# Gating on unnormalised rows: centred gate weights, a mean column and one rstd chain in a GNN and expert kernel

## What is computed

```
x = x + gnn(layernorm(x))          # two graph convolutions, batch norm over rows, + identity, relu
n = layernorm(x)                   # (x - mean) / sqrt(var + 1e-5), per row
logits = n @ gate_w + gate_b       # 256 x 8
p = softmax(logits); the two largest of 8 keep their p as weights, the others 0
x = x + sum over experts e of p[e] * (gelu(n @ W1[e] + b1[e]) @ W2[e] + b2[e])
```

## Time and profile before

| | |
|---|---|
| runs timed | 2361.3, 2357.24, 2357.84 us; median 2357.84 |
| profiled execution | 2363.68 us, its span 2361.9 us |
| busy | TensorE 82%, GpSimd 70%, VectorE 40%, ScalarE 18% of the span |
| memory traffic | 438.37 MB, 186 GB/s |

### The profile page before, as it was taken

How to read it: one execution, slowest core, us unless ns; L and a number is a source line. 1 busy time by engine, 2 the same in 40 slices (tenths; PEclk the granted TensorE clock), 3 DMA queues, 4 the chain that set the end, 5 groups by cost and what they waited for, 6 DMA issues and landing times.

```text
span 2361.9 us, 30351 instructions
## 1 busy us (share of the span) xinstructions
PE 1928.7 (82%) x8786; PEld 1400.5 (59%) x8787; DVE 933.1 (40%) x2598; ACT 423.6 (18%) x1137; POOL 1650.7 (70%) x1651
## 2 busy tenths in 40 slices
PE   1044592999999997867999999999983838999998
PEld 1044351666566665644666666666652828999997
DVE  7999310222222234422223232333237793333332
ACT  1800100000000001100000000000004673444443
POOL 0777777777777777775777777777756556666675
PEclk6555796999999999977999999999986559999999
DMA  9994542666666654444666656665672246888895
GB/s 325 342 333 130 191 125 55 201 197 206 190 198 206 201 159 149 149 118 145 197 188 192 194 186 194 187 197 182 194 234 80 78 146 174 214 208 210 209 215 127
DMA packets 289701, 438.37 MB, mean 186 GB/s; under 512 B 41634, under 2 KB 225163, under 8 KB 289451
## 3 DMA queue, kind: packets, MB, share of 16 engines
q1 hardware_dynamic: 207979, 268.31, 34.9%
q0 software_dynamic: 79872, 166.48, 27.5%
q10 hardware_dynamic: 1728, 2.13, 0.3%
HBM read 341.71 MB, written 96.51 MB: 186 GB/s over the span
## 4 chain that ended last, share of the span: by engine, by line
POOL 54%; issue 18%; PE 16%; DVE 7%; DMA 3%; ACT 1%; SPq 0%; POOLq 0%; DVEq 0%; ACTq 0%
POOL arena L597 43%; POOL pair_weights L582 11%; PE psum L1724 7%; PE psum L1732 6%; DMA out_dram<-ACC 2%; PE psum L1715 1%; DVE edge_cols L1248 1%; DVE stats L1254 1%; DVE X L1251 1%; ACT ACC L816 1%; DVE ACC L1368 1%; DMA arena<-conv_rows,edge_cols 1%; PE psum L1674 0%; PE psum L1508 0%; DVE ACC L1243 0%
## 5 line engine op out<-in xcount | busy, mean ns | idle before, releaser
L597 POOL DMA_INDIRECT arena<-conv_rows,edge_cols x1064 | 1019.9, 959 | 340.7 <-issue 324.0
L1549 PE MATMUL psum<-arena,X 128*128 128x448 f32 x1960 | 821.5, 545 | 41.0 <-DMA arena<-pair_weights 28.0
L1599 PE MATMUL psum<-arena 128*128 128x256 f32 x2128 | 583.8, 391 | 113.4 <-DMA arena<-conv_rows,edge_cols 109.2
L1599 PEld LDWEIGHTS psum<-arena 128*128 128x128 f32 x2128 | 401.7, 195 | 333.1 <-issue 275.1
L1549 PEld LDWEIGHTS psum<-arena,X 128*128 128x128 f32 x1960 | 375.3, 192 | 267.2 <-issue 218.5
L1178 DVE TENSOR_TENSOR ACC<-ACC,psum 128x256 f32 x76 | 32.1, 422 | 910.4 <-PE psum L1567 910.4
L582 POOL DMA_INDIRECT pair_weights<-scale_b,mean_b x252 | 257.0, 1020 | 132.8 <-issue 76.5
L1157 DVE TENSOR_SCALAR arena<-iota,edge_cols 128x128 f32<-128x128 f32 x1064 | 281.2, 359 | 0.4 <-DVE ACC L1084 0.2
L663 POOL DMA_INDIRECT out_dram<-ACC x105 | 166.5, 1586 | 103.8 <-DMA out_dram<-ACC 86.5
L746 ACT ACTIVATE arena<-psum 128x256 f32<-128x256 f32 x76 | 29.0, 382 | 1033.4 <-PE psum L1599 1033.4
L1724 PE MATMUL psum<-ACC,arena 128*128 128x128 f32 x1680 | 205.7, 275 | 0.2 <-DVE ACC L1395 0.2
(11 more groups left out here) (307 smaller groups left out, 1375.1 us busy)
## 6 DMA issues: line engine op xcount, KB each, us to landing
arena<-pair_weights SPq DMA_DIRECT2D x469, 224.0 KB, 3.4
arena<-in_L_ffn_W_dram SPq DMA_DIRECT2D x113, 512.0 KB, 7.5
pair_weights<-zeros SPq DMA_DIRECT2D x5, 10976.0 KB, 73.1
arena<-conv_rows,edge_cols POOLq DMA_INDIRECT x1064, 2.9
conv_rows<-X SPq DMA_DIRECT2D x13, 896.0 KB, 5.9
X<-in_x_dram SPq DMA_DIRECT2D x12, 896.0 KB, 11.2
rows_for_experts<-ACC SPq DMA_DIRECT2D x7, 910.0 KB, 4.3
out_dram<-X SPq DMA_DIRECT2D x6, 896.0 KB
```

The costliest lines, as they stand in the source:

```text
L597: pool.indirect_dma_start(G[:, n * D:(n + 1) * D], None, y_tab[layer], bass.IndirectOffsetOnAxis(srcT[:, t:t + 1], 0)).then_inc(gathered[n ...
L1549: ins = m.matmul(bank(6 + c, BW), X[:, t * D + c * P:t * D + (c + 1) * P], table, start=(t == 0), stop=(t == NT - 1))
L1599: ins = m.matmul(bank(2 * (k % 2), D), S[:, n * P:(n + 1) * P], G[:, n * D:(n + 1) * D], start=(j == 0), stop=(j == GT - 1))
```

## The change

`SCALED` goes from 4 to 3. The `bn_stats`, `bn_aggr`, root, reciprocal and normalisation per chunk go away, and so do their tiles. TensorE transposes the rows of `X` as they are, after `lb_used`. The gate weights are centred (for each expert, the mean over the 256 features is taken off each weight; the sum over features is made by TensorE against `ones`) and get a ninth column of 1/256, so that a row times them gives the eight products of the centred row and the row's mean. ScalarE squares each tile of `X` into scratch columns of `arena` and sums along the row (`accum_out`, into `ssq`). After `logit_done` one chain on VectorE makes variance = sum/256 - mean^2 for all 49 tiles, one root on ScalarE, and the products are multiplied by 1/root before the bias is added. The row numbers of the four empty adds move into column 1 of `flag_i`, written by GpSimd just before them.

```diff
-SCALED = 4
+SCALED = 3
...
+        no_row = flag_i[:, 1:2]
...
+        NC = NX + 1
+        gate_mean = sb("gate_mean", KC * NC)
+        squares = [G[:, 4 * KC * H + n * D:4 * KC * H + (n + 1) * D] for n in range(12)]
...
-                g.iota(no_row[:, :], [[0, 1]], base=NP + P, channel_multiplier=1)
...
+                chain(g.iota(no_row, [[0, 1]], base=NP + P, channel_multiplier=1))
                 for u in range(4):
...
                 norm_x(1)
                 for c in range(NCH):
-                    tiles = slice(c * CH, (c + 1) * CH)
-                    act.wait_ge(var_set, c + 4)
-                    a.activation(rstd[:, tiles], rstd[:, tiles], ACT.Sqrt).then_inc(sd_set, 1)
-                    if c:
-                        copy_turned(c - 1)
-                    act.wait_ge(ln2_set, c + 1)
-                    for q in range(c * CH, (c + 1) * CH):
-                        a.activation(acc[:, :, q * P:(q + 1) * P],
-                                     X[:, q * D:(q + 1) * D].rearrange("p (c n) -> p c n", c=KC), ACT.Identity,
-                                     bias=nmr[:, q:q + 1], scale=rstd[:, q:q + 1]).then_inc(n_ready, 1)
+                    act.wait_ge(lb_used, c + 1)
                     if c + 2 < NCH:
                         norm_x(c + 2)
+                    if c < NCH - 1:
+                        copy_turned(c)
+                    for q in range(c * CH, (c + 1) * CH):
+                        if q >= 12:
+                            act.wait_ge(squared, q - 11)
+                        a.activation(squares[q % 12], X[:, q * D:(q + 1) * D], ACT.Square,
+                                     accum_out=ssq[:, q:q + 1]).then_inc(squared, 1)
+                act.wait_ge(var_set, 4)
+                a.activation(rstd[:, :], rstd[:, :], ACT.Sqrt).then_inc(sd_set, 1)
...
+                for c in range(KC):
+                    v.scalar_tensor_tensor(out=gate_mean[:, c * NC:c * NC + NX], in0=bank(6, NX * HC + NX)[:, NX * HC:],
+                                           scalar=-1.0 / D, in1=gw[:, c * NX:(c + 1) * NX], op0=ALU.mult, op1=ALU.add)
+                    v.memset(gate_mean[:, c * NC + NX:(c + 1) * NC], 1.0 / D)
...
-                    chain(v.scalar_tensor_tensor(out=xc, in0=ring[:, n0:n0 + CH * D], scalar=0.0, in1=xc,
-                                                 op0=ALU.max, op1=ALU.add))
-                    for j in range(CH):
-                        ins = v.bn_stats(stats[:, 6 * j:6 * j + 6], xc[:, j * D:(j + 1) * D])
-                    ins.then_inc(lb_used, 1)
-                    ...
+                    v.scalar_tensor_tensor(out=xc, in0=ring[:, n0:n0 + CH * D], scalar=0.0, in1=xc,
+                                           op0=ALU.max, op1=ALU.add).then_inc(lb_used, 1)
...
+                dve.wait_ge(squared, NT)
                 dve.wait_ge(logit_done, 1)
-                tt(by_tile(prob), bank(2, T8).rearrange("p (t e) -> p t e", e=NX), per_expert(gb), ALU.add)
+                gated = bank(2, NT * NC).rearrange("p (t e) -> p t e", e=NC)
+                chain(v.tensor_copy(nmr[:, :], gated[:, :, NX]))
+                tt(mask[:, :], nmr[:, :], nmr[:, :], ALU.mult)
+                chain(v.scalar_tensor_tensor(out=rstd[:, :], in0=ssq[:, :], scalar=1.0 / D, in1=mask[:, :],
+                                             op0=ALU.mult, op1=ALU.subtract))
+                v.tensor_scalar(rstd[:, :], rstd[:, :], 0.0, LN_EPS, ALU.max, ALU.add).then_inc(var_set, 1)
+                dve.wait_ge(sd_set, 4)
+                chain(v.reciprocal(mask[:, :], rstd[:, :]))
+                tt(by_tile(prob), gated[:, :, 0:NX], per_tile(mask), ALU.mult)
+                v.tensor_copy(rstd[:, :], mask[:, :])
+                v.scalar_tensor_tensor(out=nmr[:, :], in0=nmr[:, :], scalar=-1.0, in1=mask[:, :], op0=ALU.mult, op1=ALU.mult)
+                tt(by_tile(prob), by_tile(prob), per_expert(gb), ALU.add)
...
                 pe.wait_ge(ld_const, 16 * 10)
+                for c in range(KC):
+                    m.matmul(bank(6, NX * HC + NX)[:, NX * HC:], ones[:, :], gw[:, c * NX:(c + 1) * NX],
+                             start=(c == 0), stop=(c == KC - 1))
...
                 def turn_normed(c, j):
                     q = c * CH + j
-                    pe.wait_ge(n_ready, q + 1)
+                    if j == 0:
+                        pe.wait_ge(lb_used, c + 1)
                     if c:
                         pe.wait_ge(n_copied, q - CH + 1)
                     for k in range(KC):
-                        ins = m.transpose(turned(j)[:, k * P:(k + 1) * P], acc[:, k, q * P:(q + 1) * P], ident[:, :])
+                        ins = m.transpose(turned(j)[:, k * P:(k + 1) * P], X[:, q * D + k * P:q * D + (k + 1) * P], ident[:, :])
                     ins.then_inc(n_turned, 1)
...
-                        m.matmul(bank(2, T8)[:, q * NX:(q + 1) * NX], acc[:, k, q * P:(q + 1) * P],
-                                 gw[:, k * NX:(k + 1) * NX], start=(k == 0), stop=(k == KC - 1))
+                        m.matmul(bank(2, NT * NC)[:, q * NC:(q + 1) * NC], acc[:, k, q * P:(q + 1) * P],
+                                 gate_mean[:, k * NC:(k + 1) * NC], start=(k == 0), stop=(k == KC - 1))
```

More of the change, by code:

```diff
@@ L221, in gnn_ffn @@
         tile_at = sb("tile_at", FT)
-        no_row = sb("no_row", 1, I32)
         W1g, W2g = sb("W1g", KC * D), sb("W2g", KC * D)
@@ L229, in gnn_ffn @@
         deg, dinv, mask, rstd, nmr, sc, nb = [sb(n, NT) for n in ("deg", "dinv", "mask", "rstd", "nmr", "sc", "nb")]
-        stats, mv = sb("stats", CH * 6), sb("mv", NT * 2)
         ln = sb("ln", 2 * D)
@@ L287, in gnn_ffn @@
         ln_ready, lb_ready, lb_used = [sem(n) for n in ("ln_ready", "lb_ready", "lb_used")]
-        ln2_set = sem("ln2_set")
-        n_ready, n_turned, n_copied, logit_done = [sem(n) for n in ("n_ready", "n_turned", "n_copied", "logit_done")]
+        squared = sem("squared")
+        n_turned, n_copied, logit_done = [sem(n) for n in ("n_turned", "n_copied", "logit_done")]
         lmax_set, exp_done = sem("lmax_set"), sem("exp_done")
@@ L665, in scatter_add @@
                                             compute_op=ALU.add).then_inc(added_out[u], 16)
+                chain(g.iota(no_row, [[0, 1]], base=NP + P, channel_multiplier=1))
                 for u in range(4):
-                    pool.indirect_dma_start(out, bass.IndirectOffsetOnAxis(no_row[:, 0:1], 0), zeros[:, :], None,
+                    pool.indirect_dma_start(out, bass.IndirectOffsetOnAxis(no_row, 0), zeros[:, :], None,
                                             bounds_check=N - 1, oob_is_err=False,
@@ L1057, in _ @@
                 v.tensor_copy(b1e[:, :], bank(6, NX * HC)[:, 0:NX * HC])
-                mean, var = [mv[:, :].rearrange("p (t k) -> p t k", k=2)[:, :, k] for k in range(2)]
+                for c in range(KC):
+                    v.scalar_tensor_tensor(out=gate_mean[:, c * NC:c * NC + NX], in0=bank(6, NX * HC + NX)[:, NX * HC:],
+                                           scalar=-1.0 / D, in1=gw[:, c * NX:(c + 1) * NX], op0=ALU.mult, op1=ALU.add)
+                    v.memset(gate_mean[:, c * NC + NX:(c + 1) * NC], 1.0 / D)
                 dve.wait_ge(moments_set, 1)
```

## The result

The changed kernel takes 2340.56 us in the median (2338.86 to 2342.84, 4 runs) beside 2358.91 for the kernel before (2357.24 to 2361.3, 4 runs): a ratio of 0.9925, 95% interval 0.991 to 0.994. It is 17.7 us faster by the ratio; forecast were 10.8, and the median lies 0.4 us under the low end of the range. The profiled execution took 2340.80 us (span 2339.1) in place of 2363.68, 22.9 less.

A forecast was written before the change was run, and what follows sets the result against it. GpSimd's gathers and pair writes were taken to hold most of the chain, GpSimd's turns with VectorE the gate stage. -13.3 at the logits plus 2.5 for the rstd chain, -10.8 off 2357.84, gave 2347.0 us; range 2341 to 2354.

The forecast's parts named there:

- Turns set the pace: Gate stage, chunks 1 to 6: GpSimd's turns with VectorE's tensor operations give 11.2 us a chunk, gaining 3.8 us.
- Strict turns: Gate-stage rival: GpSimd's whole pitch and VectorE's whole time exclude each other, 12.3 us a chunk, 2353.6 us; chance 0.10.
- looser ones: Gate-stage rival: more undisturbed GpSimd turns, pace falls to TensorE's 10.1 us a chunk, 2341.5 us; chance 0.10.
- ScalarE under the pace: Gate stage: norm_x, copies and seven squares at 0.60 us sum to 9.8 us a chunk, under 11.2; nothing waits.
- Rival 4: Gate stage: ScalarE's seven squares become the pace, deciding from 0.80 us a square; about 2363 us; chance 0.03.
- TensorE under the pace: Gate stage: transposes, first copy and 28 product records (6.14 us) take 10.1 us a chunk, under 11.2.
- The last chunk starts at once: End of gate stage: chunk 6's transposes follow the last relu directly, logits 9.35 us later; 9.5 us gained.
- The rstd chain: After the logits: variance, clamp, root, reciprocal, product and bias take 3.1 us in place of 0.6, costing 2.5.
- clamp 0.21: VectorE's clamp of the variance before the root, after the logits, priced at 0.21 us.
- Edges: Program start and empty adds: small added instructions and the moved row-number iota are hidden, costing nothing.
- Handing on: Stages after the logits pass the gain on; the rival that they do not gave 2354 to 2358 us, chance 0.05.
- rival 3: Tail costs more: exposed table load +1.3 to +2.6 us, later expert-stage clock rise; 2348 to 2351 us; chance 0.15.

The follow-up runs named there:

- experiment 6: The changed kernel with SCALED = 0 instead of 3, so VectorE scales all 7 tiles and GpSimd none: 2334.17 us, ratio 0.9892 to the kernel before.
- experiment 12: The changed kernel with each ScalarE square and row sum made twice: last relu ends at 78.1 and logits stand at 87.3 us after `bet`, as in the changed kernel.
- Experiment 4: The changed kernel with the row numbers moved back to their own tile, written at the start, leaving the gate redesign alone: 2352.15 us, ratio 0.9972 to the kernel before.
- experiment 1: The kernel before, unedited, run and profiled again on one chip with the others: 2360.12 us, ratio 1.0002.

## Why the prediction was right in its stage and short in its sum

- *Turns set the pace.* Right. Forecast 11.2 us a chunk, measured 11.24; L1253 of chunk 6 at 74.0 after `bet` where 1864.2 - 1790.5 = 73.7 was forecast. A VectorE half of 512 columns beside GpSimd lasts 1.21 us, 0.08 of it over the next one's start, which is the forecast 1.13. Pace gained 3.5 of 3.8. Strict turns (12.3) and looser ones (10.1) both fell; experiment 6 confirmed it for another number of turns.
- *ScalarE under the pace.* Right, with room: a square with its sum comes each 0.40 us, not 0.60, since the read of the sum overlaps the next square (40 squares busy for 16.1 us). Rival 4 was to decide from 0.80 us; in experiment 12 a tile's two squares took 0.93, the work of a chunk passed the pace, and over the five chunks that have a `norm_x` still nothing reached the path.
- *TensorE under the pace.* Right: 28 product records took 6.14 us at a granted clock of 0.50, in two chunks 3.31 and 3.91 at 0.64 and 0.66. Those of chunk 5 ended 0.8 us before the last relu, a narrow margin.
- *The last chunk starts at once.* Right: 9.3 us from the last relu to VectorE's first step behind the logits where 9.35 was forecast, and the logits 13.3 us earlier, as forecast.
- *The rstd chain, +2.5.* Too small: the reduce starts 4.95 us after VectorE's first step in place of 0.6, so +4.4. The step that failed is "clamp 0.21", which measured 1.99. The prediction looked at the engines that the chain uses and not at the one released by the same semaphore: GpSimd's iota, which stood in the trace of before. With 0.19 for it the chain is 3.15 us, where 3.1 was forecast. The table load was hidden: it ended 1.28 us after 1866.59, at 1867.87, ahead of the exponent at 1869.7.
- *Edges.* The failed step is "One iota leaves the program's start ..., hidden": correct for the iota's own 0.12 us, and wrong for what its absence does to the 1316 transfers behind it, 1064 x 8.0 + 252 x 12.0 ns = 11.5 us by the means (958.6 to 950.5 and 1019.7 to 1007.7). Nothing in the rows of before could price it, and the range had no case for a gain ahead of the stage.
- *Handing on.* Nearly: 8.9 us at the reduce, 8.5 at the end. In the expert stage the first 16 products took 3.77 us in place of 2.94, as the clock stood at 0.50 over 1933 to 1937. Before, it rose 2 us after the first of them, now 4.5 us. This is the part of rival 3 that came.

The terms as measured, -13.3 + 4.4 + 0.4, make -8.5 us for everything behind `bet`. Experiment 4, which has this half alone, gives -6.6 by its ratio (-9.7 to -3.8), and also -6.6 in the profiles against experiment 1 (`bet` to the end, 568.7 to 562.1 us), where the clock was kinder to the kernel before. The row numbers gave -13.0 alone (-17.0 to -9.2). So the forecast of -10.8 was too large for the half that it explained, by the clamp, and left out the other half.

## What to carry to other kernels

Where GpSimd and VectorE share a stage, count their turns and not their busy shares: work without a turn (here the moments) hides beside GpSimd, and a tile moved from GpSimd to VectorE can speed the stage. When a long GpSimd instruction and a short VectorE chain are released by the same semaphore, put the long one ahead of the wait if its tile is free. And before an edit to a kernel with a thousand small GpSimd transfers is credited or blamed, compare the median of one transfer before and after, since an instruction added or removed far ahead of it may move it, as one iota did here.

## What was not expected of the hardware

- GpSimd's indirect transfers take one of three sets of durations by the program around them: 953, 949 or 946 ns a gather, 967, 962 or 958 a pair write, the same in every profile of one kernel. Between the first and the last that is 11 us here, 0.5% of the whole time. An instruction of 0.12 us at the program's start switches it, an unused tile of one column in SBUF does not; why is open.
- A GpSimd iota that reads nothing held a 49-column `tensor_scalar` of VectorE for 1.8 us, while a PSUM copy and two instructions with two SBUF inputs passed beside it in 0.21 us each.
- The stage before the change was worth 3.1 us more or less between two profiles of one kernel, mostly 6.14 or 3.29 us for the same 28 product records, at a granted clock of 0.50 or 0.61 over the 16 us around them.
